# In a GRU scan of 128 steps, the product of z and the old state goes to TensorE as one fp32 matmul per gate

## What is computed

```
Z = sigmoid(xz + H @ Whz.T + bhz)
R = sigmoid(xr + H @ Whr.T + bhr)
H_tilda = tanh(xh + R * H @ Whh.T + bhh)
H_new = Z * H + (1.0 - Z) * H_tilda
```

## Time and profile before

| | |
|---|---|
| median of 3 runs | 267.89 us (267.61 to 268.12) |
| the profiled execution's own time | 267.96 us |
| its span, first to last instruction | 266.2 us |
| mean granted TensorE clock | 0.987 |
| PE (matmul) busy | 239.1 us, 90%, 3114 matmuls |
| PEld (weight load) busy | 174.2 us, 65%, 3114 loads |
| DVE (VectorE) busy | 225.7 us, 85%, 1540 instructions |
| ACT (ScalarE) busy | 127.7 us, 48%, 698 instructions |
| POOL (GpSimd) busy | 15.7 us, 6%, all in the first slices |

### The profile page before, as it was taken

One profiled execution on the slowest core, in us unless ns is written; L12 is line 12 of the kernel. 1 busy time (PEld: TensorE's weight loads), 2 busy tenths in 40 slices (PEclk: granted clock), 3 DMA queues, 4 the chain that ended last, 5 costly groups with the idle time before them and its releaser, 6 DMA issues.

```text
span 266.2 us, 8917 instructions
## 1 busy us (share of the span) xinstructions
PE 239.1 (90%) x3114; PEld 174.2 (65%) x3114; DVE 225.7 (85%) x1540; ACT 127.7 (48%) x698; POOL 15.7 (6%) x29
## 2 busy tenths in 40 slices
PE   7999889999889998999989998999888888988896
PEld 6887666658665676567665676667665565655586
DVE  3779999998999889988999889989889887788763
ACT  3355654654455444654456444654455444344432
POOL 4872000000000000000000000000000000000000
PEclk9999999999999999999999999999999999999959
DMA  7900000000000000000000000000000000000000
GB/s 253 347 9 4 0 4 2 0 4 0 4 23 0 4 2 20 5 2 0 4 22 0 4 4 18 5 2 0 5 22 1 2 2 1 22 1 4 2 20 22
DMA packets 3372, 5.65 MB, mean 21 GB/s; under 512 B 568, under 2 KB 2128, under 8 KB 3328
## 3 DMA queue, kind: packets, MB, share of 16 engines
q1 hardware_dynamic: 2848, 4.24, 4.5%
q10 hardware_dynamic: 432, 0.74, 0.8%
q0 software_dynamic: 48, 0.10, 0.1%
HBM read 4.03 MB, written 1.05 MB: 19 GB/s over the span
## 4 chain that ended last, share of the span: by engine, by line
PE 49%; DVE 31%; ACT 11%; issue 7%; DMA 1%
PE ZH L971 7%; DVE rh_p L742 7%; PE R L970 7%; ACT R L450 7%; PE R L971 7%; PE ZH L970 6%; DVE m_p L779 6%; DVE zh_p L751 3%; ACT ZH L481 3%; DVE rh_p L747 3%; DVE zh_p L745 2%; DVE rh L743 2%; DVE zh L749 2%; PE F L908 2%; PE L L978 2%
## 5 line engine op out<-in xcount | busy, mean ns | idle before, releaser
L450 ACT ACTIVATE R<-R 128x16 f32<-128x16 f32 x128 | 21.5, 168 | 64.5 <-PE R L971 62.5
L481 ACT ACTIVATE ZH<-ZH 128x16 f32<-128x16 f32 x128 | 21.5, 168 | 55.5 <-PE ZH L971 54.7
L971 PE MATMUL ZH<-rh_p,gru_hi 128*128 128x16 f16 x256 | 44.9, 176 | 0.6
L971 PE MATMUL R<-m_p,gru_hi 128*128 128x16 f16 x254 | 44.6, 176 | 0.0
L971 PE MATMUL ZH<-m_p,gru_hi 128*128 128x16 f16 x254 | 37.4, 169 | 0.0
L970 PEld LDWEIGHTS ZH<-rh_p,gru_lo 128*128 128x128 f16 x128 | 12.3, 96 | 33.8 <-DVE rh_p L742 29.0
L971 PEld LDWEIGHTS ZH<-rh_p,gru_hi 128*128 128x128 f16 x256 | 24.5, 96 | 14.3 <-DVE rh_p L747 0.2
L970 PE MATMUL ZH<-rh_p,gru_lo 128*128 128x16 f16 x128 | 21.7, 169 | 11.3 <-DVE rh_p L742 0.8
L742 DVE TENSOR_TENSOR rh_p<-R,hist 128x16 f16<-128x16 f32 x128 | 22.4, 175 | 9.5 <-ACT R L450 3.2
L779 DVE TENSOR_TENSOR m_p<-keep,ZH 128x16 f16<-128x16 f32 x128 | 21.9, 171 | 9.9 <-ACT ZH L481 8.5
L970 PE MATMUL R<-m_p,gru_lo 128*128 128x16 f16 x127 | 22.9, 181 | 6.2 <-DVE m_p L779 0.2
(11 more groups left out here) (249 smaller groups left out, 799.8 us busy)
## 6 DMA issues: line engine op xcount, KB each, us to landing
w_sb<-w SPq DMA_DIRECT2D x2, 512.0 KB, 7.9
outT<-res SPq DMA_DIRECT2D x7, 128.0 KB, 1.9
xs_sb<-xsT SPq DMA_DIRECT2D x1, 640.0 KB, 9.7
first_sb<-first ACTq DMA_DIRECT2D x1, 279.0 KB, 3.6
ffn_sb<-ffn SPq DMA_DIRECT2D x1, 256.0 KB, 3.5
ffn_sb<-ffn ACTq DMA_DIRECT2D x1, 256.0 KB, 4.6
second_sb<-second SPq DMA_DIRECT2D x1, 256.0 KB, 4.2
xs_sb<-xsT SPq DMA_DIRECT2D x1, 256.0 KB, 6.5
```

The costliest lines, as they stand in the source:

```text
L450: nc.scalar.activation(r_io, r_io, ACT.Sigmoid).then_inc(r_made, 1)
L481: nc.scalar.activation(c_io, c_io, ACT.Tanh).then_inc(cand_made, 1)
L971: return mm(out, gru_hi[:, WHR + gate, :], part, start=False, stop=low, skip_group_check=True)
```

## The change

The zh operand is no longer split. Its f16 tile zh_p and its two VectorE instructions (L745 and L751) go. TensorE reads the fp32 tile zh with the fp32 weights in gru_sb, in one matmul for r and one for z, in place of three f16 ones each. The wait for z on VectorE moves behind the low part of r·H. On TensorE the wait ahead of r's product is for zh_full (the fp32 zh) in place of zh_lo. The wait `dve.wait_ge(zh_full, ...)` stays on VectorE. The products of m and of r·H are as before.

```diff
-        zh_p = sb("zh_p", [128, 2, 2, B], F16)
...
-                    dve.wait_ge(z_made, step + 1)
-                    nc.vector.tensor_tensor(zh_p[:, q, 0, :], z_sb[:, p, :], h_old, ALU.mult).then_inc(zh_hi, 1)
                     dve.wait_ge(rh_full, step + 1)
                     nc.vector.tensor_tensor(rh_p[:, p, 1, :], rh[:, p, :], rh_p[:, p, 0, :],
                                             ALU.subtract).then_inc(rh_lo, 1)
+                    dve.wait_ge(z_made, step + 1)
                     nc.vector.tensor_tensor(zh[:, q, :], z_sb[:, p, :], h_old, ALU.mult).then_inc(zh_full, 1)
                     dve.wait_ge(zh_full, step + 1)
-                    nc.vector.tensor_tensor(zh_p[:, q, 1, :], zh[:, q, :], zh_p[:, q, 0, :],
-                                            ALU.subtract).then_inc(zh_lo, 1)
...
+            def whole_product(out, gate, part):
+
+                mm(out, gru_sb[:, WHR + gate, :], part, start=False, stop=False, skip_group_check=True)
+
...
-                        pe.wait_ge(zh_lo, step)
-                        product(r_out, 0, zh_p[:, q, 0, :])
-                        product(r_out, 0, zh_p[:, q, 1, :], low=True)
+                        pe.wait_ge(zh_full, step)
+                        whole_product(r_out, 0, zh[:, q, :])
                         pe.wait_ge(m_hi, step)
                         product(r_out, 0, m_p[:, q, 0, :])
                         pe.wait_ge(m_full, step)
-                        product(z_out, 1, zh_p[:, q, 0, :])
-                        product(z_out, 1, zh_p[:, q, 1, :], low=True)
+                        whole_product(z_out, 1, zh[:, q, :])
                         product(z_out, 1, m_p[:, q, 0, :])
```

More of the change, by code:

```diff
@@ L235, in build @@
             ("r_made", "z_made", "keep_made", "cand_made", "h_made"))
-        rh_hi, zh_hi, m_hi = sem("rh_hi"), sem("zh_hi"), sem("m_hi")
+        rh_hi, m_hi = sem("rh_hi"), sem("m_hi")
         rh_full, zh_full, m_full = sem("rh_full"), sem("zh_full"), sem("m_full")
-        rh_lo, zh_lo, m_lo = sem("rh_lo"), sem("zh_lo"), sem("m_lo")
+        rh_lo, m_lo = sem("rh_lo"), sem("m_lo")
         last_y_mm, last_y_hi, last_y_lo, last_logit_mm, last_top, last_key = (
```

## The result

The changed kernel is slower by 5.7%: ratio 1.057 to the kernel before, 95% interval 1.0531 to 1.0609. Its four executions took 282.65, 284.26, 292.05 and 293.04 us (median 288.15) against 268.0. The ratio leaves out the two longest, whose mean granted clock was 0.895 and 0.912; the profiled one (282.65, span 280.8) had 0.963. The prediction was 277.4 us, range 273.0 to 281.0: right in sign, too low.

The account below looks back on a forecast made before the run. The prediction took the GRU step's own latency as the bound. From 267.96 us it added 6.2 (z), 3.5 and 0.4 (TensorE behind), less 0.4 and 0.2 (VectorE): 277.5, stated as 277.4 us, range 273.0 to 281.0.

Parts of the forecast that it names:

- What bounds the kernel: Whole GRU step: its own latency of 1.88 to 1.89 us, whatever DVE does; TensorE has 0.09 us spare after m_full.
- The product for z: TensorE between m_full and r's last load, 104 ordinary steps: fp32 pair adds 0.06 us each, 6.2 us.
- The product for r: TensorE ahead of m's high part, ordinary steps: 0.145 us more, just hidden in 0.16 us of idle time.
- TensorE behind: 20 steps in k of 1 and more, 256-column matmuls right before r's zh product: 0.17 us each, 3.5 us.
- VectorE: L745 and L751 go, not what the step waits for: 0.4 us back in all, 0.2 once in the first step.
- L779 still 0.03 after tanh: Sign for the forecast being right: VectorE's m product still starts 0.03 us after tanh ends.
- 0.4 us expected from L747: r·H's low part on VectorE starts 0.003 us a step earlier without L745, bounds 0 and 1.3 us in all.
- the first step's 0.2: First step: r's low part no longer stands behind L745's 0.21 us wait for z; 0.2 us back, once.
- Rival (c), the clock: Blocks' sparse steps: longer steps make PE emptier and the clock falls; 10 us over a quarter of steps, 287 us; chance 0.06.
- (a): z's pair: first fp32 load done ahead of the wait for m_full, ordinary steps cost nothing; 271.2 us, chance 0.07.
- (b): VectorE's relief decides: L751 and L745 are time on the path, 13.3 us; sum 264.7 us, chance 0.04.
- (d): fp32 pair at 16 columns is short between f16 matmuls and fits the spare 0.09 us; 267.3 us, chance 0.02.

Follow-up runs that it names:

- the f16 experiment: Changed kernel with zh kept in f16 and one f16 matmul with the high weights per gate in place of the fp32 one: 271.18 us, ratio 1.014.
- only r: Kernel before with only r's zh product as one fp32 matmul, z's left in f16 parts: 268.62 us, ratio 1.0041.
- the last clock runs: Changed kernel with one more unread 256-column matmul wherever keep_streaming has room in blocks 1 to 7: 283.43 us; changed kernel again, same chip: 287.75 us.

## Why the prediction was wrong

- *What bounds the kernel* held: the step's latency, 0.09 us of slack behind m_full, DVE's work off the path. The trace after and the f16 experiment show it.
- *The product for z*: right mechanism, 0.07 for 0.06 a step. *The product for r* was hidden as said (only r: 1.88 us). *TensorE behind*: 0.18 to 0.19 for 0.17, but in 14 of the 20 steps; the six at t = 5 cost little more than an ordinary one. Too low in one term and too high in the other, they come to 9.8 us where 9.5 was summed: that this is so near is in part luck.
- *VectorE* is the step that failed first. "They aren't what the step waits for" is true of L745 and L751 as work; but L751 carried a wait, and taking it away made two waits meet on m's first product. The term was put at 0.6 us back; it cost 3.2 us, which one moved line gives back. The sign named for right, "L779 still 0.03 after tanh", is the one that broke. The 0.4 us expected from L747 didn't come (0.29 after L741 as before), and of the first step's 0.2 came 0.02 (2.14 to 2.12 us). DVE's busy time fell by 17.5 us and not by 40: the instructions that went overlapped their neighbours, which start 0.09 us apart.
- *Rival (c), the clock*, was given 0.06 and a price of 10 us or, within the range, 1 to 2 us in the last block. The sum had nothing for it, and that is the second step that failed. Falls came in single stretches of two to five steps, 2.9 us in the profiled execution's loop. The executions at 291 to 293 are up to 10 us longer, and why is not shown (see the last clock runs). The sign that the prediction had named for it, a clock under 1 before 240 us, was seen.
- *Rivals (a), (b), (d)* fall: the load comes 0.05 behind m in fp32 (84.57, 84.62), m's high part starts 0.94 after r·H as before, and r's last load comes 0.07 later behind m's start (84.32 to 84.90, before 100.22 to 100.73).

The sum was 277.5 for the profiled execution. With 0.3 for the products and 3.2 for the wait it is 281.0, the edge of the range. With the clock's 2.9, less 1.2 behind the loop, it is 282.7, against 282.65 measured. Either of the two failed steps alone would have stayed within the range. This split was made after the runs, so that it closes is no test of it.

## What to carry to other kernels

In this kernel a matmul's price was its slots in TensorE's order at the place where it stands. An fp32 product with 16 columns cost 0.00 us a step in idle time and 0.07 ahead of the last product of a chain. It gained 0.08 at a chain's end, where it made a three-step split needless. Before removing an instruction, look at which waits it carries and what will carry them. In a kernel whose clock is held up by filler matmuls, a longer step is also a sparser one: check the granted clock of the sparsest stretch, not the mean.

## What the runs showed of the hardware

- A wait that had to be an instruction of its own, ahead of a product that carries another, made it start 0.10 us after its releaser in place of 0.03.
- With z's product issued twice, the clock fell at 30.3 us, after 3.36 of 3.50 us busy, and stayed at 1.2 GHz for 362 us, although PE was busy for 4.00 of 4.00 us in a window there.
- At 1.2 GHz the changed kernel's step is 2.40 us for 1.95.
- A second pair of fp32 loads with 16 moving columns made the step 0.22 us longer, 0.11 a load, as the loads of fp32 matmuls follow each other in the earlier trace rows.
